# A graph attention layer whose edge groups keep their own maxima and store node rows, in place of a running window of sums

## What is computed

```python
def attention(x, src, dst, W, att_src, att_dst, bias):   # 8 heads of 16 channels
    xp = (x @ W).reshape(N, 8, 16)
    a_src = einsum('nhc,hc->nh', xp, att_src)
    a_dst = einsum('nhc,hc->nh', xp, att_dst)
    e = leaky_relu(a_src[src] + a_dst[dst], 0.2)
    m = segment_max(e, dst)
    ex = exp(e - m[dst])
    denom = segment_sum(ex, dst)
    alpha = ex / (denom[dst] + 1e-16)
    out = segment_sum(xp[src] * alpha[:, :, None], dst).reshape(N, 128)
    return out + bias
x = layernorm(x + attention(x, ...))
```

## Time and profile before

| | |
|---|---|
| median of three runs | 9356.58 us (9354.81 to 9357.62) |
| the profiled execution, its span | 12999.9 us |
| the profiled execution's own time outside the profiler | none is recorded; the three runs are other executions |
| instructions in the span | 294862 |
| DMA packets and bytes | 962709, 999.47 MB |

### The profile page before, as it was taken

The page is one execution under the profiler, slowest core; times in us unless marked ns, Lnnn a source line. Parts: engine busy times, 40 slices in busy tenths (PEclk is TensorE's granted clock), DMA queues, the critical chain, the costliest instruction groups (busy, mean ns, idle before and its releaser), DMA issues. The chain is left out here.

```text
span 12999.9 us, 294862 instructions
## 1 busy us (share of the span) xinstructions
PE 9231.9 (71%) x88712; PEld 7531.3 (58%) x88762; DVE 6869.4 (53%) x25269; ACT 3183.5 (24%) x9441; POOL 5674.7 (44%) x5790
## 2 busy tenths in 40 slices
PE   5977777777777777677777774888873555555555
PEld 5866667776766667634454453666662444444443
DVE  8964444444444444456666665555544555555555
ACT  5841111112111111241111123111113233222223
POOL 3534444442444444305555551444442555555552
PEclk8888888888888888789999996888886555555555
DMA  1013333333333333462222223333332111111113
GB/s 50 28 47 90 91 89 89 88 90 105 90 89 90 89 88 90 95 217 69 67 67 66 67 70 110 101 104 102 101 94 70 39 39 39 39 39 39 39 39 61
DMA packets 962709, 999.47 MB, mean 77 GB/s; under 512 B 141701, under 2 KB 861933, under 8 KB 962093
## 3 DMA queue, kind: packets, MB, share of 16 engines
q1 hardware_dynamic: 774502, 616.47, 17.1%
q0 software_dynamic: 174720, 364.70, 12.9%
q10 hardware_dynamic: 13255, 16.19, 0.4%
HBM read 858.52 MB, written 144.69 MB: 77 GB/s over the span
## 5 line engine op out<-in xcount | busy, mean ns | idle before, releaser
L497 POOL DMA_INDIRECT ring<-att_table,idx x1592 | 1556.3, 978 | 1307.7 <-ACT idx L484 715.5
L1225 PE MATMUL psum<-ring 128*128 128x128 bf16 x21276 | 1547.8, 226 | 784.6 <-issue 766.3
L1225 PEld LDWEIGHTS psum<-ring 128*128 128x128 bf16 x21276 | 1281.3, 101 | 984.9 <-issue 927.9
L1162 DVE TENSOR_SCALAR ring<-sel,iota_col 128x640 bf16<-128x640 bf16 (+1 forms) x1576 | 487.0, 369 | 2368.2 <-remote 1627.6
L1240 PE MATMUL psum<-state 64*128 64x128 f32 x14112 | 1479.8, 356 | 208.9 <-issue 206.7
L1240 PEld LDWEIGHTS psum<-state 64*128 64x128 f32 x14112 | 1318.1, 261 | 345.7 <-issue 330.0
L1148 POOL DMA_INDIRECT ring<-gcn_table,idx x980 | 932.3, 951 | 1300.6 <-ACT idx L1197 996.0
L1679 POOL DMA_INDIRECT state<-rel_table,state x1120 | 1071.1, 956 | 981.8 <-ACT state L1779 657.6
L1148 POOL DMA_INDIRECT ring<-rows,idx x980 | 933.7, 953 | 1289.0 <-ACT idx L1197 993.2
L1169 DVE TENSOR_SCALAR state<-iota_row,state 128x128 f32<-128x128 f32 x5488 | 1457.2, 356 | 0.0
L1394 POOL DMA_INDIRECT state<-hyp_table,state x784 | 755.8, 964 | 855.3 <-ACT state L1471 650.6
(11 more groups left out here) (447 smaller groups left out, 15814.7 us busy)
## 6 DMA issues: line engine op xcount, KB each, us to landing
ring<-xparts SPq DMA_DIRECT2D x1332, 192.0 KB
ring<-srow SPq DMA_DIRECT2D x544, 128.0 KB
sel<-drow SPq DMA_DIRECT2D x394, 160.0 KB
sel<-drow SPq DMA_DIRECT2D x394, 128.0 KB
rel_table<-tout SPq DMA_DIRECT2D x98, 512.0 KB, 2.6
ring<-att_table,idx POOLq DMA_INDIRECT x1592
ring<-rows SPq DMA_DIRECT2D x56, 448.0 KB
xparts<-state SPq DMA_DIRECT2D x28, 672.0 KB, 3.6
```

Of the source, the lines that this page charges most:

```text
L497: pool.indirect_dma_start(out=ring[:, u, k, 0:width], out_offset=None, in_=table, in_offset=bass.IndirectOffsetOnAxis(ap=idx[:, u, k:k + 1 ...
L1162: ins = nc.vector.tensor_scalar(reach[u % 2][:, t, :], wanted[u], at[:, :], None, ALU.is_equal)
L1225: last = nc.tensor.matmul(rowsP[v][:, j * P:(j + 1) * P], reach[v][:, t, j * P:(j + 1) * P], xwin[u][:, t, i, :], start=(t + i == 0), stop ...
```

## The change

**Attention.** Each group keeps its own maxima, so that no group reads what another one wrote. Its sums, denominators, target logits and maxima form rows of 152 words (ROW7), which SP stores: the row of the group's first node to firsts, the 127 others to body. The source rows are 144 words (ROW6: features, source logits, target logits), gathered into 7 buffers (TURN); the waits between the gathers of a group and the 3 groups beyond the last go. The starts of nodes come by DMA from starts8, the target logits of the window from att_table, both by SP, 5 groups ahead. Each group's stores wait for the landing of the stores before. ACT's window copies, write-back and exponent of the factors, PE's turns of starts, windows and results, and DVE's new_maxima and merge go; ACT's sums_out comes in. A block shared_nodes behind the pass merges the first rows of the groups into body. edge_by_edge is for unsorted inputs and runs one neutral step else; attention_setup takes the place of start_rounds and round_setup.

**Elsewhere.** edge_tables clears body and writes startrow eight times over into starts8, ahead of the first piece's load; the first block of the program stores startrow and turns one list less into columns. project("att") makes rows of 144 words with one kind of matmul, without L2307 and L2250. The last norm loads the rows of body beside its input, and has no copies on ACT and no turns on PE. The hyperbolic norm no longer clears state on POOL.

```diff
...
+ROW6 = D + 2 * HEADS
+DEN, AD, ME = D, D + HEADS, D + 2 * HEADS
+ROW7 = D + 3 * HEADS
+TURN = 7
+PAIR = (0, 1, 0, 1, 0, 1, 2)
...
@@ edge_tables, SP @@
+                    sp.dma_start(body.rearrange("(t p) c -> p t c", p=P),
+                                 no_sums.unsqueeze(1).to_broadcast([P, NPAD // P, ROW7])
+                                 ).then_inc(sem("kept1"), 16)
+                    for h in range(HEADS):
+                        sp.dma_start(starts8.rearrange("(c h) p -> c h p", h=HEADS)[:, h, :], startrow
+                                     ).then_inc(sem("kept1"), 16)
                     sp.sem_inc(sem("kept0"), 16)
                     sp.sem_inc(sem("parts"), 2)
                     load(0, 0)
...
+                    sp.wait_ge(sem("kept1"), 16 + 16 * HEADS)
@@ residual_norm @@
                         sp.dma_start(tiles(xblk[:, u, :]), rows_of(res, b)).then_inc(sem(f"xin{u}"), 16)
+                        if kind == "att":
+                            sp.dma_start(tiles(tout[:, u, 0:BT * ROW5], ROW5), rows_of(body, b)[:, :, 0:ROW5]
+                                         ).then_inc(sem(f"xin{u}"), 16)
...
-                        if kind == "att":
-                            nc.scalar.activation(xT[0:STW, u, :], state[0:STW, cols], ACT.Copy)
-                        nc.scalar.activation(stage[:, u, :], acc[:, cols], ACT.Copy).then_inc(sem("staged"), 1)
...
-                                    if kind == "att":
-                                        last = nc.tensor.transpose(psum[:, 4 + u, t * STW:(t + 1) * STW],
-                                                                   xT[0:STW, u, t * P:(t + 1) * P],
-                                                                   ident[0:STW, 0:STW])
@@ project @@
-                        if kind == "att":
-                            act.wait_ge(sem("proj"), b + 1)
-                            nc.scalar.activation(state[AD:AD + HEADS, cols], pblk(1)[0:HEADS, :], ACT.Copy
-                                                 ).then_inc(sem("saved"), 1)
...
                             pe.wait_ge(sem("tB"), b + 1)
-                            pe.wait_ge(sem("saved"), b + 1)
                             for t in range(BT):
-                                nc.tensor.matmul(psum[:, 4 + t // 3, (t % 3) * ROW5:(t % 3 + 1) * ROW5],
-                                                 xT[:, u, t * P:(t + 1) * P], Watt[:, 0:ROW5],
-                                                 start=True, stop=True)
-                            for o, w in ((0, 512), (512, BW - 512)):
-                                last = nc.tensor.matmul(psum[0:HEADS, 2 + o // 512, 0:w],
-                                                        Watt[:, ROW5:ROW5 + HEADS],
-                                                        xT[:, u, o:o + w], start=True, stop=True)
+                                last = nc.tensor.matmul(psum[:, 4 + t // 3, (t % 3) * ROW6:(t % 3 + 1) * ROW6],
+                                                        xT[:, u, t * P:(t + 1) * P], Watt[:, :],
+                                                        start=True, stop=True)
@@ attention @@
+        def attention_pass():
...
+                @block.gpsimd
+                def _(pool):
+                    with pool.Fori(0, TURNS) as it:
+                        for w in range(TURN):
+                            pool.wait_ge(sem("staged"), it * TURN + (w + 1))
+                            pool.sem_inc(sem("issued"), 1)
+                            for k in range(K):
+                                pool.indirect_dma_start(
+                                    out=att_rows[w][:, k, :], out_offset=None, in_=att_table,
...
+                    def load(i):
+                        n, w, _ = ahead(i, 5)
+                        if there(n):
+                            b = sp.value_load(base_i[0:1, bass.ds(n, 1)], min_val=0, max_val=NPAD - P)
+                            sp.dma_start(starts_T[w], starts8[bass.ds(n * (K * HEADS), K * HEADS), :]
+                                         ).then_inc(sem(f"l{w}"), 16)
+                            sp.dma_start(node_row[w][:, AD:AD + HEADS], att_table[bass.ds(b, P), AD:AD + HEADS]
+                                         ).then_inc(sem(f"l{w}"), 16)
+
+                    def store(i):
...
+                            sp.wait_ge(sem("rowcopy"), n + 1)
+                            sp.wait_ge(sem("stored0"), n * 32 + 32)
+                            sp.dma_start(firsts[bass.ds(n, 1), :], node_row[w][0:1, :]
+                                         ).then_inc(sem("stored0"), 16)
+                            sp.dma_start(body[bass.ds(b + 1, P - 1), :], node_row[w][1:P, :]
+                                         ).then_inc(sem("stored0"), 16)
...
+                    def sums_out(n, w):
+                        act.wait_ge(sem("slot"), n + 1)
+                        nc.scalar.activation(node_row[w][:, 0:ROW5], oW, ACT.Copy).then_inc(sem("rowcopy"), 1)
+
+                    def step(i):
+                        stage_logits(i)
+                        sel_narrow(i)
+                        weights_of_edges(i)
+                        sel_out(i)
+                        before, w, _ = ahead(i, -1)
+                        if there(before):
+                            sums_out(before, w)
+                            after, _, _ = ahead(i, TURN - 1)
+                            if there(after):
+                                stage_index(after, w)
...
+                        scan(i)
+                        select(i)
+                        alternate(edge_logits(i), node_values(i))
+                        alternate(take_last(i), messages(i))
...
+                    def step(i):
+                        turn_logits(i)
+                        turn_maxima(i)
+                        turn_selection(i)
+                        values_to_edges(i)
+                        maxima_to_nodes(i)
+                        group_sums(i)
...
+        def shared_nodes():
...
+                    for h in range(2):
+                        pool.wait_ge(sem("staged"), h + 1)
+                        pool.indirect_dma_start(
+                            out=here[h], out_offset=None, in_=body,
+                            in_offset=bass.IndirectOffsetOnAxis(ap=node_i[h], axis=0)).then_inc(sem("g0"), 16)
+                    pool.wait_ge(sem("g0"), 32)
+                    pool.wait_ge(sem("added"), 1)
+                    for h in range(2):
+                        pool.indirect_dma_start(
+                            out=body, out_offset=bass.IndirectOffsetOnAxis(ap=node_i[h], axis=0),
+                            in_=here[h], in_offset=None).then_inc(sem("g1"), 16)
+                        pool.wait_ge(sem("g1"), h * 16 + 16)
...
         def attention():
 
-            start_rounds(positions=True)
-            with nc.Fori(0, rounds_w()):
-                small_steps(lambda: nc.vector.memset(qround[:, :], 0.0))
-                with nc.Fori(0, nc.values_load(rounds[0:1, 1:2], min_val=1, max_val=P)):
-                    round_setup(0, True)
-                    attention_pass()
-                small_steps(lambda: nc.vector.tensor_scalar(wround[:, :], wround[:, :], float(WIN), None,
-                                                            ALU.add))
+            attention_setup()
+            edge_by_edge()
+            attention_pass()
+            shared_nodes()
```

More of the change, by code:

```diff
@@ L2077, in one @@
                                              ).then_inc(sem("sdev"), 1)
-                        if kind != "hyp" and not isinstance(it, int):
+                        if kind in ("gcn", "rel") and not isinstance(it, int):
                             stage_block(b + 2, u)
@@ new lines, in maxima_to_nodes @@
+                    def maxima_to_nodes(i):
+                        n, w, _ = ahead(i, 2)
+                        if there(n):
+                            pe.wait_ge(sem("runlast"), n + 1)
+                            pe.wait_ge(sem("targets"), n)
+                            for k in range(K):
+                                for p in range(3):
+                                    last = nc.tensor.matmul(nM[:, k, :], sel_b[PAIR[w]][:, k, :],
+                                                            last_parts[:, k, p, :],
+                                                            start=(p == 0), stop=(p == 2))
+                            last.then_inc(sem("nodemax"), 1)
@@ new lines, in group_sums @@
+                    def group_sums(i):
+                        n, w, _ = ahead(i, 0)
+                        if there(n):
+                            pe.wait_ge(sem("msg"), n + 1)
+                            pe.wait_ge(sem("rowcopy"), n)
+                            for k in range(K):
+                                last = nc.tensor.matmul(oW, sel_of[w][:, k, :], att_rows[w][:, k, 0:ROW5],
+                                                        start=(k == 0), stop=(k == K - 1))
```

(1 more changed line is left out.)

979 lines of the change are left out of this document (477 added, 502 removed).

## The result

The kernel after takes 9474.7 us (median of four runs, 9469.8 to 9476.2), the kernel before 9357.1: a ratio of 1.0118, 95 % interval 1.0105 to 1.0131. It is slower by 118 us; the prediction had it faster by 65, with a range that ended at 9410.

A forecast was written before the change was run, and what follows sets the result against it. Plain attention loop perhaps bound by gathers (10.0 us per group), the serial chain (8.55) close under. Terms −77 + 43 − 4 − 28 + 27 − 24 = −63 on 9356.6: 9294, given as 9292; range 9090 to 9410.

The forecast's parts named there:

- About 520 us of stalls remain: Gathering passes of the kernel before: 7340 us plain time against 6820 needed at 1.25 per gather; attention's share 152 us.
- −77: Attention loop: gain from removed stalls, the middle between −153 (none left) and 0 (they lie in the gathers themselves).
- Rival (a): Gathers bound both kernels, no stall to win, pitch 1.34 us; loop gives 0, time 9370; chance 0.22.
- After: 1568 × 1.25 = 1960: Attention loop after: gathers start every 1.25 us; with about 24 us of drain and 5 of storing, 1989 us.
- edge_tables **+43: Start of the kernel: nine DMAs (14.5 MB) ahead of the first piece's load delay POOL; +43 us, bounds +20 to +100.
- Project **−28: Attention projection: without L2307 and L2250's copy, 2.0 us off each of 14 blocks; −28 us (−14 to −35).
- setup with edge_by_edge **+3: Ahead of the attention's gathers: memsets and list arithmetic that go, −15 us; edge_by_edge run once on sorted inputs, +18.
- shared_nodes **+28: New block behind the attention pass: loads, gathers, PE and DVE operations and two scatters in turn; +28 us.
- Final norm **−24: Last norm: DVE alone the bound, 7.2 us per block instead of 8.9, over 14 blocks; −24 us (−15 to −30).
- The stores "at nothing": SP's row stores in the attention loop: a group's 77 KB take 4 to 5 us of 10, hidden; priced at nothing.
- Rival (c): Attention's stores become the bound at 12 us per group, loop +239, 9610; chance 0.13 together with dearer starts or blocks.
- Rival (b): Serial chain bound the plain attention loop, with gathers at 1.0 us; loop −283, time 9090; chance 0.20.

The follow-up runs named there:

- the second profile: The kernel before, unchanged, profiled once more because the profiled execution used by the prediction was 39 % longer than the runs: 9349.1 us (one run).

## Why the prediction was wrong

Its direction and most of its size came from two steps, and both failed. (The terms give 9293.6, put down as 9292, and three times 8.55 is 25.7, not 24; nothing hangs on either.)

**"About 520 us of stalls remain; attention's share by its gathers (1592 of 5456) is 152 us."** The sum of 7340 us for the gathering passes was right (the second profile: 1303.9 + 1305.0 + 1522.5 + 1154.6 + 2021.8 = 7308). The share was wrong. The attention had the least: 2021.8 us against 1592 × 1.25 = 1990, so 32, of which 30 are the gathers' own length over 0.945 us and 2 the one wait. The other passes had the rest over 1.25 us a gather: the hyperbolic one 175 us and the typed one 122, nearly all waits, the two of the GCN 79 and 80, of which some 50 are waits and 30 the gathers' length (976 ns). So the −77 had no stalls to draw on. The disturbed profile spread waits over all passes alike, and I shared them by count for want of better; but it held the number that decides: 8.55 us for the chain against 10.0 for the gathers. By that the plain loop could have no more than a fill and a few collisions to lose. Rival (a) said so of the loop, and had 0.22; its pitch of 1.34 us for all gathers is not what the attention had (1.27).

**"After: 1568 × 1.25 = 1960", with the drain 1989.** The gathers took 2091.3, not 1960, and the drain 39.7, not 29. 132 us are the gathers' own lengthening, 114 of them on gathers that overlap a selection. With the drain the loop is 90 us longer than before's (2021.8 + 19.4), where −77 was forecast. I had written that in after "no late signal stands in a chain any more" and that gathers start every 1.25 us; the median does (1.25), the mean is 1.33, over the 1.3 that the prediction named as a sign of being wrong. I had looked at what POOL would wait for, not at whether POOL would be as fast as before, though the change put DVE's operations in another order. The drain is longer since the last stores follow at 5.93 us each; split, it is 27.8. The other sign, a profiled span that falls toward 12200, tells nothing of the change, since before's own span was 9347.3 the second time.

The others by their steps:

- edge_tables **+43**: measured +37.8 at the first gather, from a wait of 44.4. Right in size and mechanism (DMA engines full at about 300 GB/s, forecast 318), and the place is the cause: moved, 36.5 come back.
- Project **−28**, setup with edge_by_edge **+3**: together −25 foretold, −46.3 measured. Project was undersized: the pair of blocks in the earlier trace rows has 6.3 us, but every third step of before is 7.9. From the first copy of target logits to the last, 13 steps, before takes 86.8 us; the same 13 steps of after take 46 us by the starts of its matmuls (3.4 to 3.5 each, the first 4.5), 3.1 off a block and not 2.0. The step from the last copy of the projection to the first gather is 23.4 us for 26.6.
- shared_nodes **+28**: 9329.5 to 9360.4, 30.9 us.
- Final norm **−24**: 7.0 us per block as foretold (7.2); 133.2 to 113.2 us, −20.
- The stores "at nothing": right for time, wrong as a size. They take 5.9 us per group of 10.7, not 4 to 5, and POOL waited for nothing in the loop; they show at the end. Rival (c), which had them as the bound, is out: from 10 us on it would decide, and it stayed at 5.9.
- Rival (b), gathers at 1.0 us without a profile, is out: gathers stand at 1.25 in all profiles, and the span of a profile that is not disturbed is the run's time.

**Not foretold and not explained:** the typed pass, which the change doesn't touch, is 33 us longer in after (1555.5 for 1522.5) and 1553 to 1563 in every variant of it, while POOL's gathers there keep their 949 ns and its waits for ACT grow from 148.5 to 180.6. The granted clock is 0.98 in both. DVE's idle time at the head of each turn of that loop, ahead of L1693 (L1570 in after) and put down to nothing but "issue", grows from 97.9 to 121.4 us over 27 turns; that is 23.5 us, but whether POOL's waits come from it, and why it grows, stays open. The tensors in SBUF and DRAM lie elsewhere in the two programs; whether that is it was not tried. It is a quarter of the loss, and none of the edits took it back.

**What of the mechanism stays open.** Shown is that the selections lengthen the gathers (operand moved to PSUM: −101 us), that in this kernel they do so only right behind the scan (apart from it or ahead of it: −83 and −84), and that a wait behind each takes it away even there (−84). Not shown is why the place behind the scan matters, and why in before the scan in front of the row holds only 21 gathers over 1.25 us, seven of them over 1.6. The length of the row, its being unbroken and its moment within a gather don't tell the orders apart, as the rows above show. Nor does the number of DVE's register instructions for the selections that run during the row: 4 to 6 in most rows of after, with an excess of 0.5 to 0.7 us per row, and 5 or 6 in most rows with the selections ahead of the scan, with 0.11 to 0.16. The seven buffers and SP's stores and loads, which before doesn't have, were not tried by themselves.

## What to carry to other kernels

Where the gathers of one engine bound a loop, ask of a change not only what that engine waits for, but what runs beside it: a row of DVE operations from SBUF to SBUF can make the bound itself slower while every wait goes away. An operand in PSUM gave all of it back here, and a gap between the operations or other work dealt in between them all but some 10 us, at no cost that shows. Clears and copies that are needed late belong behind the loads that are needed first on the same queue, and before sharing out an unexplained time by count, look for the stage's own floor and chain: they said here that the loop had nothing to give.

## What the runs showed that was not expected

- In one kernel, the same eight selections cost the gathers that overlap them 113.8 us right behind the scan, 22.9 ahead of it and 6.8 apart from it; a row twice as long, with gaps, costs 24.2.
- The packets of a store of 127 partitions (75.4 KB) run one behind the other for 4.6 us, and the store repeats every 5.93 us; cut as 112 + 15 partitions they all start within 1.3 us.
- One profiled execution had a span 39 % over the run's time, with event after event late on PE's signals; the next profile of the same kernel, 9347.3 us, had none of it. A profile whose span and run differ that much should be taken for its durations alone, not for its waits.
